# Values scaled among the rotation's turns, scores ahead of maxima and packing, and four smaller moves in an eight-batch transformer block

## The chip, the cores and the metric

One core of a Trainium2 chip runs the program. The metric is the device time of one execution in microseconds. The engines are TensorE (PE in the profile, its weight loads PEld), VectorE (DVE), ScalarE (ACT), GpSimd (POOL) and SyncE (SP), which issues nearly all transfers.

## What is computed

The input x is 8 x 512 x 512, float32. Four layers follow, each added to x after a layer norm of its result:

```python
x = x + ln(lightning_attention(ln(x)))   # 16 query heads, 4 key/value heads of 128, rotation, decay per head
x = x + ln(feed_forward(ln(x)))          # silu(gate) * up, inner 2048, weights (w - 128) * scale
x = x + ln(softmax_attention(ln(x)))     # 32 query heads, 8 key/value heads of 16, rotation, causal
x = x + ln(row_ffn(ln(x)))               # works on the last row, then sigmoid gate over all rows, layer norm
```

The first attention has, per head, q k^T times a table exp(-lam (i - j)), plus a state carried from block to block. The second is the usual softmax attention, with the row maximum subtracted.

## The kernel before, in words

**Precision.** Most products are made of three: every operand is kept as a high and a low part in fp32r. ScalarE copies the high part, VectorE or GpSimd subtracts it from the full value for the low part (`low`, line 1292 on VectorE), and `product` on TensorE multiplies high x high, low x high, high x low.

**Batches are pipelined.** Iteration n (0 to 8) does the first attention of batch n, then its feed-forward; between the pieces of the feed-forward stands the second attention of batch c = n-1; the gate product of batch d = n-2 stands in the first attention. Iteration 8 has no first attention and no feed-forward, and the row network and the last norm come behind it. Each engine's program is written out by hand in one order, with semaphores between them: `fill(bank, emptied)` on TensorE waits until the previous reader of a PSUM bank is through.

**First attention.** Four groups g, each of one key head and four query heads. A group begins with five turns u = 0..4 (keys, then four query heads). In a turn TensorE projects into P0 or P1 (`project`), ScalarE swaps the halves (`swapped`), GpSimd multiplies by the sine table (`sines`, L863), VectorE multiplies by the cosine table (`cosine`, L1344), makes the previous turn's low part (`rope_low`, L1292) and adds the sines (`rotate`, L1350). Behind u = 3 TensorE transposes the key back (`keys_back`), into bank Y0 for g = 0 and E0 otherwise; ScalarE copies it out (kv_hi). For g = 0 `all_values` follows, in banks Y0 and O. Then come the blocks of ten jobs: VectorE scales something into pf (L1407; two buffers), ScalarE copies the high part pT_hi, GpSimd subtracts the low part pT_lo (L875). Jobs 0 and 1 are values times decay (`scaled_values`), read by the state; jobs 2 to 7 are scores times decay (banks T0, T1), 8 and 9 the part from the state. A score product waits for the pf that emptied its bank. In g >= 1 TensorE does the output products of the group before (banks Y0, O; y_acc) ahead of its blocks.

**Fronts and start of the feed-forward.** Then norms, transposes and the q, k, v products of the second attention; VectorE rotates its queries (part 0) and keys (part 1) by `rotate_pairs(c, part, t)`, t = 0..3. The feed-forward has 48 slots, four quarters q of 12. In slots i = 0..7 of a quarter (i = s mod 12) gate (even, bank P0) and up (odd, bank P1) products take turns; ScalarE makes tanh of the gate product, VectorE `silu` (L1568) and `hf` (L1578); in slots 8 to 11 come the down products (Y0, added to y_acc). `product_out(n, s)` is VectorE's part of slot s.

**Second attention, in steps.** From slot 5 five steps stand in three slots: two, two, one. Eight groups of five quads of heads: step i makes scores of quad i mod 5 (`scores`, L2095, banks T0 and T1), VectorE adds the causal mask to the corner (L1551) and takes the maxima (L1558, row_max); only then are T0 and T1 free. A step that needs it also does: `maxima` (L2117, group g at step 6 + 5g, transposes row_max into a spare bank, VectorE copies it as maxT, L1526, SyncE sends it on into QT), `pack_queries` (L2073, step 5g - 2), `pack_keys` (L2081, step 5g - 1), `values_back` (L2134, step 17 + 5g; VectorE divides, rden and y1). Scores in the other orientation with exp (`probs`, L1160), a mask by GpSimd (L897), and products with the values (L2126) come at the start of a step. `layout_high` and `layout_low` put the rotated queries and keys of a group into q_pack and k_pack, two low parts each, on VectorE, at step 5g - 5. The spare bank is P0 in slots with i >= 8, where no gate product runs, and Y0 otherwise. Maxima stand in slots 8, 11, 14, 17, 20, 23, 26 and 29.

**Order of a step on TensorE before:** values, transposed scores, half a slot of feed-forward, maxima, pack_queries, pack_keys, values_back, scores.

**n = 0** also prepares the weights. Each piece is loaded raw, split into high and low (ScalarE, VectorE), and for later batches written to a scratch in DRAM. `first_pieces` gives each piece its place; slots 24 to 31 have the eight pieces of wo1 and of the gate beside eight units and four down pieces per quarter. The fourth quarter has four down pieces.

Of the kernel before, what the change touches and what calls it, by code (L numbers as in the profile page):

```python
# [163 lines left out]
def first_pieces():  # L164
# [98 lines left out]
def build(nc, x, raw_f, raw_i, gate_scale, up_scale, down_scale, rope1_tables, causal, identity_b,  # L263
# [8 lines left out]
    with ExitStack() as ctx:  # L272
# [130 lines left out]
        def keys_bank(g):  # L403

            return "E0" if g else "Y0"
# [428 lines left out]
        def _(pool):  # L834
# [19 lines left out]

            def rope(n, g):
                for u in range(NU):
# [8 lines left out]
                    if g == 2 and u and n:  # L865
                        rstds("pc", n - 1, u - 1)

            def blocks(n, g):
                for k in range(NJOB):
                    lin = (n * KV0 + g) * NRING + k  # L870
                    if k < NRING and lin >= 4:
                        pool.wait_ge(pv.sem, lin - 3)
                    pool.wait_ge(*p_hi.need(n, g, P_HI[k]))
                    if k < NRING:
                        pool.tensor_tensor(pT[1][:, k % 4, :], pf[:, k % 2, :], pT[0][:, k % 4, :].bitcast(F32),  # L875
                                           ALU.subtract).then_inc(*p_lo.hit(n, g, k))
                    else:
                        h = slice(2 * (k - NRING), 2 * (k - NRING) + 2)
# [3 lines left out]
            def clear_pads(c):  # L882
# [6 lines left out]
                pool.memset(k_pack[:, :, 1::2, HD1 + 1:32].bitcast(F32), 0.0).then_inc(*pads.hit(c, 5))  # L889

# [9 lines left out]
            for n in range(NB + 1):  # L900
# [45 lines left out]
                for s in range(SLOTS):  # L946
# [65 lines left out]
        def _(act):  # L1012
# [44 lines left out]

            def rope(n, g):
# [11 lines left out]
                copy(kv[0][:, :], ps[keys_bank(g)][:, :]).then_inc(*rope_hi.hit(n, g, KEYS_AT))  # L1070
# [20 lines left out]
            def blocks(n, g):  # L1091
                for k in range(NJOB):
# [19 lines left out]
                    lin = (n * KV0 + g) * NRING + k  # L1112
                    if k < NRING:
                        if lin >= 4:
                            act.wait_ge(pv.sem, lin - 3)
                        act.wait_ge(*p_f.need(n, g, P_F[k]))
                        copy(pT[0][:, k % 4, :], pf[:, k % 2, :]).then_inc(*p_hi.hit(n, g, P_HI[k]))
# [172 lines left out]
        def _(dve):  # L1290
# [67 lines left out]
            def rope(n, g):  # L1358
                d = n - 2
                dve.wait_ge(*tables_in.need(n))  # L1360
                for u in range(NU):
# [3 lines left out]
                    rotate(n, g, u)  # L1365
                    if g == 0 and d >= 0 and u in (1, 3):
# [139 lines left out]
            def layout_low(c, g):  # L1506
                dve.wait_ge(*q_hi.need(c, g))
                dve.wait_ge(*rot_sum.need(c, 1, NT - 1))
                q_ = q_pack[:, :, :, :].rearrange("p t h e -> p (t h) e")
                low(q_[:, :, 2 * HD1:3 * HD1], R_q[:, g, :, :].rearrange("p t (h d) -> p (t h) d", h=4), q_[:, :, 0:HD1])\  # L1510
                    .then_inc(*q_lo.hit(c, g))
                dve.wait_ge(*k_hi.need(c, g))
                low(k_pack[:, :, 0::2, HD1:2 * HD1], R_k[:, g, :, :].unsqueeze(2).to_broadcast([P, NT, 2, HD1]),
                    k_pack[:, :, 0::2, 0:HD1]).then_inc(*k_lo.hit(c, g))

            def step(c, i):
                at = SLOT_OF[i]
                if prepare_at(i) is not None:
# [897 lines left out]
```

## Time and profile before

| what | value |
|---|---|
| median of three runs | 4074.02 us |
| runs | 4074.05, 4072.42, 4074.02 us |
| the profiled execution | 4069.46 us |
| its span | 4067.7 us |
| mean granted TensorE clock | 0.957 of full speed |
| TensorE busy | 3684.8 us, 91% |
| VectorE busy | 2525.5 us, 62% |
| ScalarE busy | 1505.8 us, 37% |
| GpSimd busy | 1359.4 us, 33% |

The span runs from the first to the last instruction of the profiled execution; its own time is 1.8 us more. Instructions are named by line and tiles: `pf<-ps_T,dec` writes pf and reads ps_T and dec. In a row of the timeline the bracket gives how long the engine stood idle before the instruction and what ended that. x2 joins two equal neighbours.

### The profile page before, as it was taken

Reading aid. Unit: us, or ns where it says so; the run is one execution under the profiler, and the core shown is the slowest. Engines: PE = TensorE matmul, PEld = TensorE weight load, DVE = VectorE, ACT = ScalarE, POOL = GpSimd, SP = SyncE. Lnnn points to the kernel's source line nnn. Section 1 sums busy time; section 2 is a strip of 40 time slices with the busy share of each in tenths; the row PEclk is TensorE's granted clock in tenths of the full one; section 3 lists DMA queues with packets and bytes.
Section 4 is the critical chain, followed back from the end, with each engine's and each line's share of the span. In section 5 each row is a group of like instructions: output and inputs, shape, how many; then the busy total and the mean of one; then the engine's idle time right before and its main releaser. Section 6 shows DMA issues by size and latency. Waiting matters only on the chain. (4 is left out here: it accounts for less than half of the span.)

```text
span 4067.7 us, 51226 instructions
## 1 busy us (share of the span) xinstructions
PE 3684.8 (91%) x18536; PEld 2706.8 (67%) x18536; DVE 2525.5 (62%) x4174; ACT 1505.8 (37%) x2349; POOL 1359.4 (33%) x1674
## 2 busy tenths in 40 slices
PE   6977999999999999999899998999999999977678
PEld 5756776677767776677767776677767776664323
DVE  6654666556674667566664766566664666466347
ACT  4422333434243433434242434434243424315124
POOL 3421452235312551245313541245223541121114
PEclk9988999999999999999999999999999999987789
DMA  6456433254324533254324533353335432332304
GB/s 249 166 215 248 175 129 135 86 205 161 135 84 161 179 122 131 99 205 153 124 94 161 184 106 137 116 204 130 125 105 190 151 134 100 114 106 73 134 14 153
DMA packets 173798, 578.99 MB, mean 142 GB/s; under 512 B 14727, under 2 KB 14983, under 8 KB 168174
## 3 DMA queue, kind: packets, MB, share of 16 engines
q1 hardware_dynamic: 169854, 568.38, 39.3%
q10 hardware_dynamic: 3696, 7.34, 0.5%
q8 instruction: 151, 2.47, 0.3%
q14 instruction: 97, 0.79, 0.1%
HBM read 490.21 MB, written 84.93 MB: 141 GB/s over the span
## 5 line engine op out<-in xcount | busy, mean ns | idle before, releaser
L1892 PE MATMUL ps_P<-XnT_hi,w_ring 128*128 128x512 f32 x3328 | 1084.7, 408 | 60.2 <-DVE silu L1568 24.5
L1892 PEld LDWEIGHTS ps_P<-XnT_hi,w_ring 128*128 128x128 f32 x3328 | 608.5, 192 | 232.1 <-issue 92.3
L1892 PE MATMUL ps_P<-XnT_lo,w_ring 128*128 128x512 f32 x1664 | 659.9, 397 | 0.0
L952 POOL TENSOR_TENSOR hT_lo<-hf,hT_hi 128x512 fp32r<-128x512 f32 x128 | 164.4, 1285 | 935.8 <-ACT hT_hi L1014 935.8
L875 POOL TENSOR_TENSOR pT_lo<-pf,pT_hi 128x512 fp32r<-128x512 f32 x256 | 326.4, 1291 | 358.2 <-ACT pT_hi L1014 358.2
L1160 ACT ACTIVATE probs<-ps_E 128x1024 f32<-128x1024 f32 x320 | 327.5, 1023 | 304.8 <-PE ps_E L2109 304.3
L1558 DVE TENSOR_REDUCE row_max<-ps_T 128x2 fp32r<-128x768 f32 (+3 forms) x448 | 400.1, 917 | 11.0
L1892 PEld LDWEIGHTS ps_P<-XnT_lo,w_ring 128*128 128x128 f32 x1664 | 318.8, 192 | 71.7
L897 POOL TENSOR_SCALAR_AFFINE_SELECT probs<-probs 128x512 f32<-128x512 f32 x256 | 160.0, 637 | 617.2 <-ACT probs L1160 616.1
L1892 PE MATMUL ps_Y<-w_big,hT_hi 128*128 128x512 f32 x896 | 332.0, 417 | 24.8 <-POOL hT_lo L952 11.3
L1551 DVE TENSOR_TENSOR ps_T<-ps_T,mask 128x512 f32<-128x512 f32 (+1 forms) x320 | 187.9, 587 | 230.8 <-PE ps_T L2095 228.9
L863 POOL TENSOR_TENSOR sines<-swapped,sinT 128x512 f32<-128x512 f32 x160 | 212.9, 1331 | 221.3 <-ACT swapped L1014 213.4
L1014 ACT ACTIVATE pT_hi<-pf 128x512 fp32r<-128x512 f32 x256 | 157.2, 630 | 290.3 <-DVE pf L1407 290.3
L1014 ACT ACTIVATE swapped<-ps_P 64x512 f32<-64x512 f32 x320 | 189.8, 593 | 202.4 <-PE ps_P L1892 117.6
L1407 DVE TENSOR_TENSOR pf<-ps_T,dec 128x512 f32<-128x512 f32 x256 | 175.2, 689 | 133.8 <-POOL pT_lo L875 103.3
L1892 PEld LDWEIGHTS ps_Y<-w_big,hT_hi 128*128 128x128 f32 x896 | 169.3, 189 | 99.8 <-issue 17.1
L2095 PE MATMUL ps_T<-KT,QT 64*128 64x256 f32 (+3 forms) x1024 | 166.1, 382 | 72.7 <-DVE row_max L1558 71.5
L1014 ACT ACTIVATE hT_hi<-hf 128x512 fp32r<-128x512 f32 x128 | 80.8, 631 | 311.5 <-DVE hf L1578 311.5
L1568 DVE SCALAR_TENSOR_TENSOR silu<-silu,ps_P 128x512 f32<-128x512 f32 x128 | 87.6, 684 | 167.8 <-ACT silu L1235 167.8
L1344 DVE TENSOR_TENSOR roped<-ps_P,cosT 128x512 f32<-128x512 f32 x160 | 110.3, 689 | 121.9 <-ACT swapped L1014 120.7
L2095 PEld LDWEIGHTS ps_T<-KT,QT 64*128 64x128 f32 x1024 | 84.4, 191 | 149.9 <-DVE row_max L1558 103.5
L2109 PE MATMUL ps_E<-QT,KT 64*128 64x512 f32 (+2 forms) x896 | 154.9, 389 | 25.3 <-ACT probs L1160 25.2
(330 smaller groups left out, 7505.0 us busy)
## 6 DMA issues: line engine op xcount, KB each, us to landing
w_ring<-split_dram SPq DMA_DIRECT2D x412, 512.0 KB, 3.5
w_big<-split_dram SPq DMA_DIRECT2D x64, 2048.0 KB, 7.7
dec<-decay SPq DMA_DIRECT2D x32, 1024.0 KB, 5.0
split_dram<-w_ring SPq DMA_DIRECT2D x58, 512.0 KB, 4.4
split_dram<-w_big SPq DMA_DIRECT2D x36, 512.0 KB, 4.3
wo1w<-split_dram SPq DMA_DIRECT2D x8, 2048.0 KB, 7.6
gatew<-split_dram SPq DMA_DIRECT2D x7, 2048.0 KB, 10.8
X<-raw_f SPq DMA_DIRECT2D x46, 256.0 KB, 4.2
```

Source lines behind the costliest of these rows:

```text
L863: pool.tensor_tensor(sines[:, u % 2, :], swapped[:, u % 2, :], sinT[:, :], ALU.mult)\
L875: pool.tensor_tensor(pT[1][:, k % 4, :], pf[:, k % 2, :], pT[0][:, k % 4, :].bitcast(F32), ALU.subtract).then_inc(*p_lo.hit(n, g, k))
L897: pool.affine_select(out=corner, in_=corner, compare_op=ALU.is_ge, fill=0.0, base=0, pattern=[[0, 4], [1, P]], channel_multiplier=-1).then ...
L952: pool.tensor_tensor(hT[1][:, m % IC, :], hf[:, m % 2, :], hT[0][:, m % IC, :].bitcast(F32), ALU.subtract).then_inc(*h_lo.hit(n, m))
L1014: return act.activation(out_, in_, ACT.Copy)
L1160: act.activation(dst[:, heads_of(ns), :].rearrange("p (b n) i -> p b n i", n=len(ns)), psE[:, :, :].rearrange("p b (n i) -> p b n i", n=le ...
L1407: dve.tensor_tensor(out_, in_, table, ALU.mult).then_inc(*p_f.hit(n, g, P_F[k]))
L1551: dve.tensor_tensor(corner.rearrange("p b n (k s) -> p b (n k) s", s=P) if nh == 1 else corner, corner.rearrange("p b n (k s) -> p b (n k) ...
L1558: last = dve.reduce_max(row_max[:, g % 2, block, heads_of(ns)].rearrange("p (b n) -> p b n", n=len(ns)), psT[:, :, at:at + len(ns) * w].re ...
L1892: last = pe.matmul(dst, stat[s_], mov[m_], start=first_ and k == 0, stop=last_ and k == n - 1, **kw)
L2095: last = pe.matmul(dst[q][:, at + m * w:at + (m + 1) * w], QT[rows_, g % 3, pair, cols(block)], KT[rows_, g % 3, 0:w], start=True, stop=True)
L2109: last = pe.matmul(dst[q][:, at:at + nh * w].rearrange("p (h i) -> p h i", i=w), KT[rows_, g % 3, cols(j)], QT[rows_, g % 3, ns[0]:ns[0] + ...
```

## The change

Six edits:

1. At n = 0 the pieces of wo1 and of the gate go from slots 24 to 31 to slots 38 to 45.
2. `keys_back` uses bank E0 also for g = 0, as long as n < 2.
3. For g >= 1 VectorE's `scaled_values` 0 and 1 stand behind the rotations of turns 2 and 3; ScalarE's and GpSimd's parts of jobs 0 and 1 stand in turns 3 and 4. The blocks then begin with VectorE's two accumulations. GpSimd's roots for "pc" are divided over groups 2 and 3 (turns 1 and 2).
4. `layout_low` runs on GpSimd, in the same steps.
5. In a step TensorE issues `scores` ahead of maxima, pack_queries, pack_keys and values_back. VectorE does mask corner and maxima ahead of the maxT copy and of values_back's division.
6. VectorE's first `product_out` (silu of the first gate product) stands behind the first of the four key rotations instead of behind all four.

```diff
-        if 24 <= s < 28:
-            at.append(("o", s - 24))
-        if 28 <= s < 32:
-            at.append(("g", s - 28))
+        if 38 <= s < 42:
+            at.append(("o", s - 38))
+        if 42 <= s < 46:
+            at.append(("g", s - 42))
...
-        def keys_bank(g):
+        def keys_bank(n, g):
-            return "E0" if g else "Y0"
+            return "E0" if g or n < 2 else "Y0"
...
@@ GpSimd, rope(n, g) @@
-                    if g == 2 and u and n:
-                        rstds("pc", n - 1, u - 1)
+                    if g and u >= 3:
+                        job_low(n, g, u - 3)
+                    if g >= 2 and u in (1, 2) and n:
+                        rstds("pc", n - 1, 2 * (g - 2) + u - 1)
...
@@ GpSimd, slots @@
+                        if s == PREPARE0:
+                            layout_low(c, 0)
                         for i_ in steps_at(s):
+                            if prepare_at(i_) is not None:
+                                layout_low(c, prepare_at(i_))
                             if quad2(i_):
                                 mask_group(c, i_)
...
@@ ScalarE, rope(n, g) @@
+                    if g and u >= 3:
+                        job_high(n, g, u - 3)
...
@@ VectorE, rope(n, g) @@
                     rotate(n, g, u)
+                    if g and u in (2, 3):
+                        scaled_values(n, g, u - 2)
...
@@ VectorE, blocks(n, g) @@
-                for k in range(2):
-                    if g == 0:
+                if g == 0:
+                    for k in range(2):
                         values_low(n, k)
-                    scaled_values(n, g, k)
-                if g:
+                        scaled_values(n, g, k)
+                else:
                     accumulate(n, g - 1, 0)
                     accumulate(n, g - 1, 1)
...
@@ VectorE, start of the feed-forward @@
                     for t in range(NT):
                         rotate_pairs(c, 1, t)
+                        if t == 0 and n < NB:
+                            product_out(n, 0)
...
@@ TensorE, step(n, c, s, i, half) @@
+                if quad1(i):
+                    scores(c, i)
                 if rows_at(i) is not None:
                     maxima(c, rows_at(i), s)
...
                 if back_at(i) is not None:
                     values_back(c, back_at(i), s)
-                if quad1(i):
-                    scores(c, i)
```

The lines with @@ say whose program follows. On VectorE the block of `if quad1(i):` (corner and maxima) moves in the same way to the head of `step`.

## Rows read from the trace of the kernel before

**Rows 1.** The page, section 1: busy us (share of the span) x instructions.

```profile
PE 3684.8 (91%) x18536; PEld 2706.8 (67%) x18536; DVE 2525.5 (62%) x4174; ACT 1505.8 (37%) x2349; POOL 1359.4 (33%) x1674
```

**Rows 2.** Waits of TensorE: who for whom, total us, times, longest.

```profile
PE ps_T L2095 <- DVE row_max L1558: 71.5, 88, 2.3
PE ps_T L1892 <- DVE pf L1407: 70.1, 54, 2.2
```

**Rows 3.** Three stretches: busy us per engine, then clock, DMA share, GB/s.

```profile
1540.00:1545.00 5.00, 4.43 (x13) 3.54 (x14) 1.70 (x4) 0.90 (x2) 1.27 (x1) 0.66 1.03 397
1629.00:1634.00 5.00, 3.27 (x20) 2.38 (x20) 3.01 (x6) 2.86 (x4) 3.09 (x4) 1.00 0.00 0
1853.00:1859.00 6.00, 4.20 (x11) 2.87 (x12) 3.35 (x5) 1.38 (x3) 4.67 (x4) 0.72 0.00 0
```

**Rows 4.** Timeline, first silu of a batch: start, duration, line, tiles, [idle before].

```profile
1535.64 0.69 ACT L1235 ACTIVATE silu<-ps_P,ghalf 128x512 f32<-128x512 f32 x1 [5.08 <-PE ps_P L1892]
...
1539.74 0.68 DVE L1568 SCALAR_TENSOR_TENSOR silu<-silu,ps_P 128x512 f32<-128x512 f32 x1
...
1540.57 0.70 PE L1892 MATMUL ps_P<-XnT_hi,w_ring 128*128 128x512 f32 x2 [2.30 <-DVE silu L1568]
```

**Rows 5.** Timeline, a group's blocks (second group of the fifth batch).

```profile
1850.49 0.69 DVE L1292 TENSOR_TENSOR qT_lo<-roped,qT_hi 128x512 fp32r<-128x512 f32 x1 [0.70 <-ACT qT_hi L1014]
...
1851.10 1.29 DVE L1407 TENSOR_TENSOR pf<-v,ident_dec 128x512 f32<-128x512 f32 x2
...
1852.66 2.49 POOL L875 TENSOR_TENSOR pT_lo<-pf,pT_hi 128x512 fp32r<-128x512 f32 x2 [4.01 <-ACT pT_hi L1014]
...
1854.80 0.50 PE L1892 MATMUL ps_T<-qT_hi,kT_hi 128*128 128x512 f32 x1 [1.90 <-DVE pf L1407]
...
1859.43 0.39 PE L1892 MATMUL ps_Y<-w_big,oT_hi 128*128 128x512 f32 x1
```

**Rows 6.** Timeline, one turn of the rotation: VectorE and GpSimd.

```profile
1879.59 1.29 POOL L863 TENSOR_TENSOR sines<-swapped,sinT 128x512 f32<-128x512 f32 x1 [1.39 <-ACT swapped L1014]
...
1880.16 1.27 DVE L1292 TENSOR_TENSOR kT_lo<-roped,kT_hi 128x512 fp32r<-128x512 f32 x1
...
1880.84 0.64 POOL L845 TENSOR_TENSOR var_eps<-moments,eps 128x1 f32<-128x1 f32 x1
...
1881.36 0.68 DVE L1350 TENSOR_TENSOR roped<-roped,sines 128x512 f32<-128x512 f32 x1
...
1882.27 0.69 DVE L1344 TENSOR_TENSOR roped<-ps_P,cosT 128x512 f32<-128x512 f32 x1 [0.24 <-ACT swapped L1014]
```

**Rows 7.** Timeline, slots 11 and 12 of a feed-forward.

```profile
1587.98 1.22 DVE L1558 TENSOR_REDUCE row_max<-ps_T 128x4 fp32r<-128x1024 f32 x1
...
1588.76 0.56 PE L2117 MATMUL ps_P<-identr,row_max 128*128 128x128 f32 x4
...
1589.26 0.50 PE L2095 MATMUL ps_T<-KT,QT 64*128 64x384 f32 x4
...
1589.72 0.67 DVE L1526 CAST maxT<-ps_P 4x512 fp32r<-4x512 f32 x1
...
1590.32 0.68 DVE L1551 TENSOR_TENSOR ps_T<-ps_T,mask 128x512 f32<-128x512 f32 x1
...
1590.53 0.70 PE L1892 MATMUL ps_P<-XnT_hi,w_ring 128*128 128x512 f32 x2 [0.49 <-DVE maxT L1526]
...
1591.03 1.29 DVE L1558 TENSOR_REDUCE row_max<-ps_T 128x2 fp32r<-128x768 f32 x2
```

**Rows 8.** VectorE on q_pack, all batches: ns min/median/max, first and last start.

```profile
L1292 DVE TENSOR_TENSOR q_pack<-R_q,q_pack x64: 412/435/1095, 633.3 to 3732.1; 128x256 fp32r<-128x256 f32 x64
```

**Rows 9.** Quarters two to four of the first feed-forward, columns as in rows 3.

```profile
289.00:331.00 42.00, 36.34 (x148) 28.27 (x147) 18.82 (x29) 11.96 (x20) 5.15 (x4) 0.96 0.61 226
331.00:388.00 57.00, 40.17 (x142) 30.13 (x142) 27.09 (x44) 16.78 (x28) 8.03 (x12) 0.85 0.72 276
388.00:425.00 37.00, 36.15 (x165) 28.75 (x164) 17.84 (x29) 9.54 (x16) 5.14 (x4) 1.00 0.51 185
```

**Rows 10.** Timeline of TensorE, the wait ahead of the first batch's values.

```profile
50.16 0.77 PE L1892 MATMUL ps_Y<-w_big,XnT_hi 128*128 128x512 f32 x1 [8.53 <-ACT kv_hi L1014]
```

More of the change, by code:

```diff
@@ L864, in rope @@
                         .then_inc(*sine_done.hit(n, g, u))
[L865 to L866 removed]
+                    if g and u >= 3:
+                        job_low(n, g, u - 3)
+                    if g >= 2 and u in (1, 2) and n:
+                        rstds("pc", n - 1, 2 * (g - 2) + u - 1)
             def blocks(n, g):
[L869 to L873, printed above, removed]
+                for k in range(2 if g else 0, NJOB):
                     if k < NRING:
[L875 to L876 removed]
+                        job_low(n, g, k)
                     else:
+                        pool.wait_ge(*p_hi.need(n, g, P_HI[k]))
                         h = slice(2 * (k - NRING), 2 * (k - NRING) + 2)
@@ L1056, in rope_high, with job_high @@
                     .then_inc(*rope_hi.hit(n, g, UNIT_AT[u]))
+            def job_high(n, g, k):
+                lin = (n * KV0 + g) * NRING + k
+                if lin >= 4:
+                    act.wait_ge(pv.sem, lin - 3)
+                act.wait_ge(*p_f.need(n, g, P_F[k]))
+                copy(pT[0][:, k % 4, :], pf[:, k % 2, :]).then_inc(*p_hi.hit(n, g, P_HI[k]))
             def rope(n, g):
@@ L1111, in blocks @@
                                 .then_inc(*o_hi.hit(n, g, h))
-                    lin = (n * KV0 + g) * NRING + k
                     if k < NRING:
[L1114 to L1117, printed above, removed]
+                        if k >= 2 or g == 0:
+                            job_high(n, g, k)
                     else:
@@ L1504, in rotate_pairs @@
                 dve.tensor_tensor(dst, dst, b_.rearrange("p (g e) -> p g e", g=KV1), ALU.add).then_inc(*rot_sum.hit(c, part, t))
[L1506 to L1514, printed above, removed]
             def step(c, i):
                 at = SLOT_OF[i]
-                if prepare_at(i) is not None:
-                    layout_low(c, prepare_at(i))
+                if quad1(i):
+                    g, x_ = quad1(i)
+                    if c * KV1 + g >= 2:
+                        dve.wait_ge(rows_mm.sem, c * KV1 + g - 1)
+                    dve.wait_ge(*pads.need(c, 0))
+                    nh = len(STEPS1[x_][0][1])
+                    corner = psT[:, :, :].rearrange("p b (n s) -> p b n s", n=nh)[:, :, :, (4 // nh - len(STEPS1[x_])) * P:512 // nh]
+                    dve.wait_ge(*score1.need(c, g, x_))
+                    dve.tensor_tensor(corner.rearrange("p b n (k s) -> p b (n k) s", s=P) if nh == 1 else corner,
+                                      corner.rearrange("p b n (k s) -> p b (n k) s", s=P) if nh == 1 else corner,
+                                      mask[:, :].unsqueeze(1).unsqueeze(1).to_broadcast([P, 2, max(nh, len(STEPS1[x_])), P]), ALU.add)\
+                        .then_inc(*corner_done.hit(c, g, x_))
+                    dve.wait_ge(*corner_done.need(c, g, x_))
+                    for block, ns, at_ in STEPS1[x_]:
+                        w = (block + 1) * P
+                        last = dve.reduce_max(row_max[:, g % 2, block, heads_of(ns)].rearrange("p (b n) -> p b n", n=len(ns)),
+                                              psT[:, :, at_:at_ + len(ns) * w].rearrange("p b (n s) -> p b n s", s=w), AX_X)
+                    last.then_inc(*max_done.hit(c, g, x_))
                 g = rows_at(i)
@@ L1745, in _ @@
                             step(c, i)
-                    if n < NB and s % 12 < 8:
+                    if n < NB and s % 12 < 8 and (s or c < 0):
                         product_out(n, s)
```

41 lines of the change are left out of this document (19 added, 22 removed).

## The prediction, on record before the changed kernel ran

> **What bounds the kernel now.** I read the page first, then the list of waits of TensorE, then single stretches of the timeline. TensorE is busy for 3684.8 us, 91% of the span, and the next engine 62% [rows 1], so only what TensorE waits for, and how fast it runs, can move the time. The waits for row_max and for pf, 70 us each, lead its list [rows 2]; the change goes at both, and at a wait for silu that comes once a batch. Second reading, the granted clock: the stretch behind the 2.30 us silu wait was granted 0.66 and that behind a 1.90 us pf wait 0.72, while behind a 1.73 us wait at 1631.15 it stayed 1.00 [rows 3]. At 2.4 GHz a mean of 0.66 means that part of the stretch ran at 1.2 GHz. The price of such a spell: 5 us x 0.34 = 1.7 us, or 6 us x 0.28 = 1.7 us [rows 3]. So a wait of about two microseconds costs itself and 1.7 us more, and one below about 1.7 us only itself.
>
> **The first silu moved up (seven batches).** tanh of the first gate product ends at 1536.33, but VectorE comes to silu at 1539.74, behind all four key rotations, and TensorE, which wants the same bank, stands 2.30 us until 1540.57 [rows 4]. The first rotation takes about 0.85 us (four lie between 1536.33 and 1539.74), so silu then runs from 1537.2 to 1537.9, ahead of 1538.27, when TensorE is ready for it. I leave 0.3 us of the wait. The three rotations behind it end 0.68 us later and have only a packing many microseconds later as reader. Gain 2.0 + 1.6 of clock = 3.6 us, x7 = **-25** (bounds -14, without the clock, and -28).
>
> **Scaled values among the turns (21 groups with g>=1).** Now a group begins when the last qT_lo is there, at 1851.18; then two scalings of 0.65, two POOL subtractions of 1.25, and only then the scaled scores that the third score product (job 4) waits for: TensorE waits 1.90 for pf and begins the outputs at 1859.43, 8.2 us after the start [rows 5]. After the change the scalings and POOL's first two subtractions stand in turns 2 to 4. What do turns have free? Per turn VectorE does a cosine 0.69, a low 1.27 and a rotation 0.68, and ahead of the next cosine, at 1882.27, it stands idle for 0.24 [rows 6]. The low is 1.27 and not 0.69 as it is when POOL is idle [rows 5, 6]: it starts at 1880.16 inside POOL's sines and ends 0.55 after these. And POOL's tiny var_eps, issued at 1880.84, lasts until VectorE's low is over. The rows read best as turns taken, one whole operation after the other, not as two slower operations. Then each of two job lows (1.25) and two scalings (0.65) goes into the queue of both engines: I set them into turns 2 to 4 and got the last low 2.7 us later than now. TensorE waits these 2.7 at the start and then no longer for pf at job 4; outputs begin 4.8 us behind the last low at full clock, or 5.8 with a half-speed spell: 7.5 to 8.5 against 8.2. That is -0.7 to +0.3 per group; the wait of 2.7 is of those that cost clock, so I take the upper half: **0** (bounds -69, if the turns' slack swallowed all but 0.15 of it, and +17, at 0.8 more per group). The Trainium skill, page "SBUF — State Buffer", section "SBUF: two separate sides", says that VectorE and GpSimd share one port pair as an exclusive lock: a VectorE operation with two SBUF inputs and a GpSimd operation that reads SBUF never overlap, the first to start keeps it to its end. By that the delay would be the 2.7 taken here, and the rule speaks against this part of the change. The trace agrees as far as it goes, with its low that ends 0.55 us behind POOL's operation. POOL's variance roots move from g=2 to g=2 and 3, same count: nothing, covered by the same turns (if not covered, 0.64 [rows 6] a few times per batch, within the bound).
>
> **Scores ahead, maxima and maxT behind.** In slot 11 the scores come at 1589.26, just after their condition, the reduction that ends at 1589.20 (1587.98 + 1.22 [rows 7]). Maxima stand ahead of them and cover that wait. Afterwards the scores can't start sooner: TensorE idles there, and maxima follow. On VectorE corner and reduction (0.68, 1.29) now come ahead of the maxT copy (0.67), which frees bank P0; the next slot's gate product needs P0. Today it waits 0.49 and starts at 1590.53. By the new order: corner 1589.8, reduction to 1591.8, maxT to 1592.5, product at 1592.6: 2.1 us later, of which the next scores' small wait gives back 0.2, and the idle above adds 0.4: 2.3. The same holds at slot 23: only in these two do maxima use P0 right before a gate product; elsewhere (slots 8, 14, 17, 20, 26, 29) nobody wants the bank at once. Packing, behind the scores, gets its operands' banks later; subtractions for it now run on POOL, twice as long per element (1.25 against 0.69 for the same shape [rows 5]), with a mask ahead of them. I add 0.25 and 0.8 for the two groups where the packing then waits on them, and take off 0.3 where a score comes sooner. Per batch: 2 x 2.3 + 1.0 = 5.6, x7 = **+39**. Each new wait is about 2.0 to 2.1, where the rows show half-speed spells [rows 3]; with chance 0.8 each, and one more at half that weight, 1.8 spells x 1.7 = 3.0 per batch, x7 = **+21**. Bounds: +10 (the packing alone) and +75.
>
> **Layout lows to POOL in the last pass.** With no feed-forward, VectorE is the bound of n=8, and 8 x 0.435 leave it [rows 8], and as many of the keys' lows, of half the elements: 5.5 us, **-5** (bounds -8 and 0). In the other batches VectorE's time for it is the gap that TensorE does not see.
>
> **Weights at n=0.** The third quarter (331:388) takes 57 us for nearly the TensorE work (40.2 us busy, against 36.3) that the second does in 42, with the clock at 0.85 [rows 9]. In it 20 weight pieces are split (8 units, 4 of the down weights, 8 of wo1 and gate), in the second 12. Eight of them (wo1, gate) go to slots 38 to 45, into the fourth quarter, which has 4 now and then 12, as the third will. If a quarter of 12 pieces costs what the second costs, the third falls to 41 or 42 us (-16 of its 57.8), and the fourth (388:425, 37 us [rows 9]) rises towards 42: +5. **-11** (bounds -14 and -6).
>
> **Bank of the first key transposes (n<2).** TensorE waits 8.53 us for kv_hi at 50.16 [rows 10], because all_values wants the same bank; with E0 it goes at once, until it needs v_lo, which VectorE gives only behind the last qT_lo of the turns. By my placing that takes back half of the wait. **-4** (bounds -7, 0); n=1: nothing, as the next wait, v_lo, ends where it did.
>
> **Sum:** -25 + 0 + 39 + 21 - 5 - 11 - 4 = **+15**. The profiled execution took 4069.5 us (span 4067.7), so 4084.5 by it; the median of the runs is 4.6 higher, 4074.0, hence **4089**.
>
> **Rivals.**
> 1. Turns absorb the scalings, faster. If only the two scalings' own 1.3 us delay the last low instead of 2.7, each block begins 1.4 earlier and keeps its clock more often (0.5): 1.9 x 21 = -40, time 4049. It decides from the point where the last qT_lo comes less than 2.4 us later than today. For it: the last low of a group runs at 0.69 [rows 5]. Against: the low and var_eps that wait out the other engine [rows 6]. Chance 0.20.
> 2. Scores first gives what it seems to promise, faster: row_max waits of 71.5 [rows 2] fall by a third, and P0's wait stays near 0.5, since the reduction finishes earlier. -24 instead of +60: 4005 to 4030. Against: the condition of the scores is met only at 1589.20. Chance 0.10.
> 3. The new waits keep the clock at 1.00, as the 1.73 us wait did [rows 3]: without the 21, 4068. Chance 0.20, no change that can be told.
> 4. The turns cost more: POOL's queue makes sines late, and both the last low and the clock suffer: +0.8 x 21, time 4106. Chance 0.12.
> 5. The main case: 0.38.
>
> **Numbers.** About 0.2% (8 us) is what a measurement of this kernel can tell from nothing: 4066 to 4082. Faster 0.30 (1, 2), same 0.20 (3), slower 0.50 (4, 5). The range reaches from rival 1's to the top of rival 4, with what the upper bound of the scores' part adds: 4040 to 4112; the likeliest case alone has 4078 to 4100.
>
> **What would show it.** Right: a wait of TensorE for maxT near 2 us at slots 12 and 24 of each batch; silu's wait at the batch's start gone, with the clock at 1.00 behind it; qT_lo of the last turn some 2.7 us later and no pf wait of 1.9; slots 12 to 23 of n=0 near 41 us. Wrong: lows of 0.69 beside POOL's new work, maxT waits unchanged, or a silu wait that has only moved to hf.

## The result, and the profile after

The changed kernel takes 4124.8 us (4118.9 to 4127.4, four runs) against 4074.0 of before in the same comparison: ratio 1.0121, 95% interval 1.0104 to 1.0139, so it is 50.8 us slower. The forecast was 4089 with a range up to 4112: the side was right, the size was not. The profiled execution took 4118.9 us (span 4117.2), 49.5 more in the span than before. Here are two lines of its page: the busy times, and the granted clock in forty equal slices of the span.

```profile
PE 3724.4 (90%) x18536; PEld 2700.7 (66%) x18536; DVE 2547.2 (62%) x4046; ACT 1505.3 (37%) x2349; POOL 1456.5 (35%) x1802
...
PEclk8989999999999999999999999999999999986789
```

Against [rows 1] TensorE's busy time is 40 us up with the same number of matmuls: they ran longer, in part because more of the time is at half speed (below). Its list of waits (who for whom, total us, times, longest):

```profile
PE ps_T L1908 <- DVE qT_lo L1318: 67.1, 24, 3.9
PE ps_T L2111 <- DVE row_max L1552: 63.0, 107, 2.3
...
PE ps_P L1908 <- DVE maxT L1561: 26.2, 14, 1.9
...
PE ps_T L1908 <- DVE pf L1435: 20.4, 20, 2.2
...
PE ps_P L1908 <- DVE silu L1584: 5.9, 7, 1.7
```

Against [rows 2] the pf wait fell from 70.1 to 20.4, as meant, and a wait for the last qT_lo stands in its place: 67.1 us in 24 waits, 2.4 to 2.9 us each in batches 2 to 8 and 3.8 to 3.9 in the first. maxT is new among the long ones at 14 x 1.87. The wait for silu is nearly gone (5.9; it was 24.5).

Where the time went is read best by stages. The table gives the length of each stretch from the starts of TensorE's projections and of the feed-forward's products, in us; a group holds its turns and its blocks, the last column of a batch runs to the next batch's first projection.

```
fifth batch        groups 1   2     3    4+fronts | quarters 1    2      3   4 and rest | sum
before              53.4  40.9  40.9  73.8        | 57.9  75.6  62.8  49.4    | 454.5
after               51.7  40.0  41.3  75.1        | 57.8  79.7  64.7  49.4    | 459.6
after, third batch  53.3  41.3  41.2  73.4        | 56.3  81.5  64.5  49.4    | 460.8

               first batch  batches 2 to 8  from there to the end | TensorE idle, half-speed time (granted clock) in 2 to 8
before            408.3        3146.0         493.9               | 173.8, 105.8 in 31 spells
after             399.6        3196.9         500.9               | 186.3, 153.6 in 36 spells
```

(In the second table batches 2 to 8 begin with the second batch's first projection and end where the last gate or up product of the eighth batch starts. The column behind runs from there to the end of TensorE's last product. A spell is a stretch at half speed without a break.) The loss lies in the second and third quarter and in the last pass; in the first quarter silu's gain and a new loss cancel out. In batches 2 to 8 TensorE idles only 12.5 us more, but 47.8 us more of its time run at half speed, which is worth half as much, 23.9. Together they are 36 of the 50.9 us. The other 15 are neither gaps nor half speed; their cause wasn't found.

### The profile page after: what moved, and what is told of

Its sections match the earlier page's. It is cut to its first block, busy times and chain, and to the rows that moved or that the text cites. A ratio compares the mean times of both kernels' runs of the same rounds, so it can differ in the third digit from the quotient of the medians.

```text
span 4117.2 us, 51225 instructions
## 1 busy us (share of the span) xinstructions
PE 3724.4 (90%) x18536; PEld 2700.7 (66%) x18536; DVE 2547.2 (62%) x4046; ACT 1505.3 (37%) x2349; POOL 1456.5 (35%) x1802
## 4 chain that ended last, share of the span: by engine, by line
PE 59%; DVE 22%; issue 7%; POOL 4%; ACT 4%; DMA 3%; SPq 1%; DVEq 0%; ACTq 0%; POOLq 0%
PE ps_P L1908 20%; PE ps_Y L1908 9%; PE ps_E L1908 6%; PE ps_T L1908 4%; PE ps_O L2142 4%; PE ps_O L1908 3%; PE ps_T L2111 3%; PE ps_E L2125 2%; DVE row_max L1552 2%; DVE roped L1376 2%; DVE ps_T L1545 2%; DVE qT_lo L1318 2%; DVE pf L1435 2%; DVE stats L1342 1%; POOL X L853 1%
## 5 line engine op out<-in xcount | busy, mean ns | idle before, releaser
L860 POOL TENSOR_TENSOR pT_lo<-pf,pT_hi 128x512 fp32r<-128x512 f32 x256 | 343.5, 1354 | 395.7 <-ACT pT_hi L1034 395.7
L871 POOL TENSOR_TENSOR sines<-swapped,sinT 128x512 f32<-128x512 f32 x160 | 225.0, 1406 | 171.8 <-ACT swapped L1034 165.8
L2125 PE MATMUL ps_E<-QT,KT 64*128 64x512 f32 (+2 forms) x896 | 163.7, 409 | 26.7 <-ACT probs L1186 26.5
L2142 PE MATMUL ps_O<-probs,V 128*32 128x512 f32 (+3 forms) x2048 | 177.0, 466 | 0.0
```

What stands on the lines that cost most here:

```text
L871: pool.tensor_tensor(sines[:, u % 2, :], swapped[:, u % 2, :], sinT[:, :], ALU.mult)\
L2125: last = pe.matmul(dst[q][:, at:at + nh * w].rearrange("p (h i) -> p h i", i=w), KT[rows_, g % 3, cols(j)], QT[rows_, g % 3, ns[0]:ns[0] + ...
L2142: last = pe.matmul(dst[at:at + 32, j * P:S], V1[:, j, g, :], probs_of(j)[:, m, :], start=(j == 0), stop=(j == NT - 1), skip_group_check=True)
```

## The experiments

Each kernel ran against the kernel before on the same chip; differences are of medians. Each took four to ten executions; the edits shown are cut to what matters (... stands for lines left out).

### The silu edit alone, and silu behind the third rotation

```diff
                         rotate_pairs(c, 1, t)
+                        if t == 0 and n < NB:     # f_only; t == 2 in f_third
+                            product_out(n, 0)
```

> The kernel before with the silu edit alone. My account: the silu wait of 2.30 us and the half-speed spell behind it go, the first quarter of the feed-forward falls from 57.9 to 54.3 us in each of seven batches: -25 us, 4049. The rival (clock spell only moves to another place): -14 us, 4060, with the first quarter at 55.9.

> The kernel before with silu behind the third key rotation instead of the first: the wait is left at 1.4 to 1.5 us instead of 2.3 or 0. If half-speed spells follow only waits near 2 us, the spell goes with it and the first quarter is near 55.4 us: -17 (4057). If the spell stays it is 57.0: -6 (4068).

The first took 4045.1, -27.5 us (ratio 0.9932, 0.9917 to 0.9947). Its first quarter is 54.3 us instead of 57.9. The second took 4056.0, -15.2 us (0.9962, 0.9950 to 0.9975), with a first quarter of 55.5. Timeline and then the stretch behind the wait (busy times of the engines, then the clock) in the second kernel:

```profile
1538.21 0.70 PE L1894 MATMUL ps_P<-XnT_hi,w_ring 128*128 128x512 f32 x2 [1.44 <-DVE silu L1568]
```

```profile
1538.00:1545.00 7.00, 6.59 (x32) 5.37 (x32) 3.56 (x11) 2.34 (x5) 1.29 (x1) 1.00 1.04 403
```

The wait is 1.44 and the clock stays at 1.00, where [rows 3] had 0.66 behind 2.30. So 0.86 of the 2.4 us that the quarter lost is wait, and the other 1.5 is the clock. This term of the forecast (-25, of it 1.6 us of clock per batch) came within 2.5 us, and here its two shares can be told apart.

The second kernel shows one thing more. Its second quarter takes 77.1 to 77.2 us in all seven batches, where before it took 75.6, and each time it holds one spell of 3.4 us that wasn't there before. In the fifth batch it comes behind a wait of 1.73 us for probs, at 2077.68; in the kernel before the same wait is 1.71, at 2085.62, and no spell follows. So in the second kernel the spell left the silu wait and another came elsewhere, as the rival in the expectation of `f_only` had it. In the first kernel none came: there the second quarter stays at 75.6.

### Scaled values among the turns, alone

> The kernel before with scaled values among the turns alone. The account by turns taken (port held by whole operations): last qT_lo 2.7 us later, blocks 3.5 us shorter, +0.4 us per group in steady batches and about +6 us at n=0: +8 to +14, 4082 to 4088. The rival (turns absorb the scalings): 1.9 us less per group, -40, 4034.

```diff
                     rotate(n, g, u)
+                    if g and u in (2, 3):
+                        scaled_values(n, g, u - 2)    # VectorE; ScalarE's and GpSimd's parts in u = 3, 4
```

It took 4072.4, -0.1 us (0.9995, 0.9985 to 1.0004): no difference, as the sum said, and below the +8 to +14 of the expectation. Why is seen in the turns of the changed kernel (fifth batch, second group, turns 2 to 4 and the head of the blocks):

```profile
1854.85 1.48 POOL L871 TENSOR_TENSOR sines<-swapped,sinT 128x512 f32<-128x512 f32 x1 [1.43 <-ACT swapped L1034]
...
1855.70 1.18 DVE L1318 TENSOR_TENSOR qT_lo<-roped,qT_hi 128x512 fp32r<-128x512 f32 x1
...
1856.29 1.74 POOL L860 TENSOR_TENSOR pT_lo<-pf,pT_hi 128x512 fp32r<-128x512 f32 x1
...
1856.80 1.77 DVE L1376 TENSOR_TENSOR roped<-roped,sines 128x512 f32<-128x512 f32 x1
...
1858.03 1.70 POOL L871 TENSOR_TENSOR sines<-swapped,sinT 128x512 f32<-128x512 f32 x1
...
1858.50 1.78 DVE L1435 TENSOR_TENSOR pf<-v,ident_dec 128x512 f32<-128x512 f32 x1
...
1861.15 1.47 POOL L860 TENSOR_TENSOR pT_lo<-pf,pT_hi 128x512 fp32r<-128x512 f32 x1 [1.42 <-ACT pT_hi L1034]
...
1861.40 1.76 DVE L1376 TENSOR_TENSOR roped<-roped,sines 128x512 f32<-128x512 f32 x1
...
1863.86 0.69 DVE L1318 TENSOR_TENSOR qT_lo<-roped,qT_hi 128x512 fp32r<-128x512 f32 x1 [0.69 <-ACT qT_hi L1034]
...
1864.61 0.50 PE L1908 MATMUL ps_T<-qT_hi,kT_hi 128*128 128x512 f32 x1 [2.59 <-DVE qT_lo L1318]
...
1866.41 0.51 PE L1908 MATMUL ps_T<-qT_hi,kT_hi 128*128 128x512 f32 x1
```

From 1854.85 to 1863.16 operations of VectorE are held up beside operations of GpSimd: GpSimd's operation at 1856.29 ends at 1858.03, and the rotation beside it, 0.68 by itself [rows 6], takes 1.77 and ends 0.54 behind it. The scaling takes 1.78 beside the sines of 1.70, and the next rotation 1.76 beside a subtraction of 1.47. The last low comes late enough that TensorE waits 2.59 at 1864.61. The pf wait of 1.90 [rows 5] is then 0.14 (the 1866.41 row follows at once). The delay was forecast at 2.7, and the waits of batches 2 to 8 are 2.4 to 2.9. Over the whole execution the mean rotation is 0.99 us, where it was 0.68. GpSimd's fuller queue is not what makes the last low late: VectorE's waits for sines are 24.3 us in all, and 24.6 before, and VectorE has no idle time between the first row shown and 1863.16. By the lock that the forecast cited from the Trainium skill ("SBUF — State Buffer", "SBUF: two separate sides") one operation waits for the whole of the other; these rows agree, except that VectorE's operation ends only about 0.55 behind GpSimd's, less than its own 0.68.

### The same on VectorE and ScalarE alone

This is the test of that reading: GpSimd's two subtractions go back to the head of the blocks, and its roots for "pc" to their old place. It was run together with the weights, layout and silu edits, beside a kernel with these three edits alone.

```diff
             # GpSimd, rope(n, g)
-                    if g and u >= 3:
-                        job_low(n, g, u - 3)
```

> Added to it: scaled values among the turns on VectorE and ScalarE alone; GpSimd's two subtractions stay at the head of the blocks. If the lock between the two engines makes the last qT_lo late, it comes only some 1.0 to 1.4 us later instead of 2.7, and the pf wait of 1.9 falls too, since GpSimd can start at once: blocks 0.5 to 1.5 us shorter each, -10 to -30 against the run without: 3980 to 4000. If VectorE's own time is at fault, the last qT_lo is 2.7 late here too and the run is no faster.

> The same without the bank of the first key transposes. My forecast gave that edit -4. The traces since show only another wait in its place (w_big 8.3 for kv_hi 8.5 at n=0, v_lo 6.5 for 2.6 + 2.0 at n=1): no difference beyond noise, or 2 us faster without it: 4010.

> All edits but the order of scores and the scaled values among the turns. If the turns' part is neutral (as it was alone), this equals the run without the order alone, 4022. If it costs once silu no longer covers the clock spell behind the last group, or at n=0, where a group took 3.9 us longer in it, this is 8 to 15 us faster: 4010.

With GpSimd left out of the turns: 3977.9 (-93.3; 0.9774, 0.9760 to 0.9789). Without the scaled values' edit: 4017.6 (-53.7; 0.9871, 0.9856 to 0.9885), and with the bank edit added 4017.7 (-53.5). So the edit is worth 40 us in this form and about nothing in the form of the change (the run below, with it, is -54.8). The second and third group of a batch take 38.7 to 38.9 and 38.1 to 38.2 instead of 39.6 to 41.3. The timeline of the fifth batch, second group:

```profile
1798.05 0.68 DVE L1370 TENSOR_TENSOR roped<-roped,sines 128x512 f32<-128x512 f32 x1
...
1798.66 0.68 DVE L1429 TENSOR_TENSOR pf<-v,ident_dec 128x512 f32<-128x512 f32 x1
...
1799.01 1.49 POOL L863 TENSOR_TENSOR sines<-swapped,sinT 128x512 f32<-128x512 f32 x1 [1.43 <-ACT swapped L1028]
...
1807.47 0.50 PE L1902 MATMUL ps_T<-qT_hi,kT_hi 128*128 128x512 f32 x1 [1.29 <-DVE qT_lo L1312]
```

The rotation and the scaling behind it run at their own 0.68; GpSimd has only its sines, and the last low makes TensorE wait 1.29 instead of 2.59. Half-speed time in batches 2 to 8 falls from 92.2 us (27 spells) to 30.7 (9), and idle time from 144.0 to 126.7: of 48 us (3108.7 to 3060.6) 17 are waits and 31 are clock. In the first batch the edit costs 9.1 in these two executions, which leaves the 40. That is the price of the forecast's first rival, with a wait near the 1.3 us that it names. The edit could have gained it, if GpSimd's part hadn't gone along.

The bank edit made no difference. In the changed kernel TensorE waits 8.25 us at the first batch for w_big (its low half is split by VectorE), where it waited 8.53 for kv_hi, and at the second batch the wait for v_lo is 6.5 instead of waits of 2.6 and 2.0.

### The order of scores, alone and split

```diff
                 # TensorE, step, in e_only and e_pe_only
+                if quad1(i):
+                    scores(c, i)
                 if rows_at(i) is not None:
                     maxima(c, rows_at(i), s)
...
                     values_back(c, back_at(i), s)
-                if quad1(i):
-                    scores(c, i)
```

In `e_only` VectorE's order changes in the same way, in `e_pe_only` it stays. In `e_maxima` TensorE's order is packing, values_back, scores, maxima, so that only maxima and the maxT copy go behind. In `e_packs` it is maxima, scores, packing, values_back.

> The kernel before with the order of scores alone, on TensorE and on VectorE. My account: first quarter +2.0, second +5 (P0's wait for maxT and the clock spell), third +2 per batch, and the pass without feed-forward +7 to +12: +70, 4144. The rival (the loss is the GpSimd lows of the packs): no more than the maxT waits, 2 x 1.4 x 7 = +20, 4094.

> The order of scores on TensorE alone; VectorE keeps maxT and the division ahead of the corner and the maxima. If the maxT copy behind corner and maxima is what costs in slots 12 and 24, the wait falls from 1.9 to about 0.9 us, its spells go, and the sum is +30 to +40 (4104 to 4114), with the last pass still +7. If it is the packing behind the scores, little changes against the run with both orders: +60 or more.

> Only maxima and the maxT copy behind the scores; packing and the division stay ahead. If P0's wait for maxT is the larger part of the loss, this has the second quarter at +5 and the sum near +60 (4133); if the packing is, it has only +2 x 1.4 us of wait and two spells of 1.7 us in a batch, +40 (4113) or less.

> Only packing and values_back (with VectorE's division) behind the scores; maxima and maxT stay ahead. Account: the 1.04 us of the query packing no longer fill VectorE's reduction, TensorE idles 0.6 us there and the packing, and the next product's wait for QT, come on top, 1.4 us in each of 8 groups plus 0.5 for the keys: up to 13 us per batch, less where slack takes it; +50 to +80 (4123 to 4153), all three quarters and the last pass. The rival: maxima carry the loss, this is +15.

Alone it takes 4188.2: **+115.6** (1.0279, 1.0264 to 1.0295), far more than the +70 that I expected. On TensorE alone 4213.6, +141.0 (1.0343, 1.0328 to 1.0359), where I expected +30 to +40. Only maxima behind: 4153.1, +76.1 (1.0191, 1.0176 to 1.0207). Only packing and values_back behind: 4119.8, +42.8 (1.0108, 1.0093 to 1.0123). The two halves add up to 118.9. I had expected about +60 for the first half and +50 to +80 for the second, each with the rival that the other half carries the loss; both halves carry it.

Maxima first. Slots 11 and 12 in the changed kernel, and the clock there (against [rows 7]):

```profile
1591.56 0.51 PE L2111 MATMUL ps_T<-KT,QT 64*128 64x384 f32 x4 [0.33 <-DVE row_max L1552]
...
1592.00 0.66 PE L2133 MATMUL ps_P<-identr,row_max 128*128 128x128 f32 x4
1592.21 0.70 DVE L1545 TENSOR_TENSOR ps_T<-ps_T,mask 128x512 f32<-128x512 f32 x1
...
1592.94 1.29 DVE L1552 TENSOR_REDUCE row_max<-ps_T 128x2 fp32r<-128x768 f32 x2
...
1594.15 0.67 DVE L1561 CAST maxT<-ps_P 4x512 fp32r<-4x512 f32 x1
...
1594.96 1.19 PE L1908 MATMUL ps_P<-XnT_hi,w_ring 128*128 128x512 f32 x2 [1.87 <-DVE maxT L1561]
```

```profile
1593.00:1601.00 8.00, 6.13 (x21) 4.26 (x18) 3.81 (x6) 2.05 (x2) 1.85 (x3) 0.57 0.45 157
1864.00:1870.00 6.00, 5.25 (x22) 3.99 (x23) 3.82 (x7) 1.78 (x4) 2.54 (x2) 1.00 0.00 0
```

Scores start when the reduction is done; maxima follow, but their copy waits in VectorE's queue for corner and reduction, and TensorE stands 1.87 us for bank P0, as forecast (2.0 to 2.1). What was not: the clock behind it. 0.57 over 8 us is 3.4 us, twice the price that I took from [rows 3]. This is one of the dearer places. Over all 14 waits for maxT, each of 1.87 us, the 8 us behind hold 4.0 us at half speed on average, worth 2.0, and behind two of them there are none. The second window holds the opposite: behind a wait of 2.59 it stayed 1.00, as behind 3 of the 21 waits for qT_lo in batches 2 to 8. Length of the wait alone doesn't tell which one is followed by a spell.

In the kernel with TensorE's order alone the copy goes first:

```profile
1624.07 0.50 PE L2095 MATMUL ps_T<-KT,QT 64*128 64x384 f32 x4 [0.35 <-DVE row_max L1558]
...
1625.27 0.68 DVE L1526 CAST maxT<-ps_P 4x512 fp32r<-4x512 f32 x1 [0.66 <-PE ps_P L2117]
...
1625.88 0.68 DVE L1551 TENSOR_TENSOR ps_T<-ps_T,mask 128x512 f32<-128x512 f32 x1
...
1626.10 0.70 PE L1892 MATMUL ps_P<-XnT_hi,w_ring 128*128 128x512 f32 x2 [0.50 <-DVE maxT L1526]
```

TensorE's wait for P0 is 0.50 as in [rows 7]. But VectorE stood idle for maxima until 1625.27, and the corner, whose scores were there at 1624.57, starts at 1625.88. The loss moved into the loop of scores and reductions: 233 us of idle time in batches 2 to 8 against 204 in `e_only`, and 104 us of waits for row_max against 53. My expectation had left VectorE's queue behind the waiting copy out. So if TensorE's order is changed, VectorE's must be too, and even then it loses.

Packing. The fourth scores of a group, first in the kernel before (packing at 1594.61, scores at 1595.58 without a wait), then in the kernel with both orders:

```profile
1594.61 0.60 PE L2073 MATMUL ps_Y<-ident_dec,q_pack 128*128 128x128 f32 x4
...
1595.58 0.49 PE L2095 MATMUL ps_T<-KT,QT 64*128 64x512 f32 x2
```

```profile
1596.16 0.51 PE L2095 MATMUL ps_T<-KT,QT 64*128 64x512 f32 x2 [0.62 <-DVE row_max L1536]
...
1596.60 0.66 PE L2073 MATMUL ps_Y<-ident_dec,q_pack 128*128 128x128 f32 x4
...
1597.10 0.60 PE L2073 MATMUL ps_P<-ident_dec,q_pack 128*128 128x128 f32 x4
...
1598.53 0.70 PE L1892 MATMUL ps_P<-XnT_hi,w_ring 128*128 128x512 f32 x2 [0.83 <-ACT QT L1014]
```

In the old order the packing, about 1 us, filled the time until the reduction was done. Now TensorE idles 0.62, packs behind the scores, and the product behind needs the bank that ScalarE is still reading: 0.83 more. It is the last pass that shows the shift of work best. Scores four to five, kernel before and changed kernel:

```profile
3692.88 0.79 PE L2095 MATMUL ps_T<-KT,QT 64*128 64x512 f32 x2
...
3696.97 0.50 PE L2095 MATMUL ps_T<-KT,QT 64*128 64x512 f32 x2
```

```profile
3738.01 0.79 PE L2111 MATMUL ps_T<-KT,QT 64*128 64x512 f32 x2 [0.45 <-DVE row_max L1552]
3738.74 1.12 PE L2089 MATMUL ps_Y<-ident_dec,q_pack 128*128 128x128 f32 x4
3739.64 1.06 PE L2089 MATMUL ps_P<-ident_dec,q_pack 128*128 128x128 f32 x4
3740.64 3.21 PE L2142 MATMUL ps_O<-probs,V 128*32 128x512 f32 x16
...
3744.35 0.40 PE L2111 MATMUL ps_T<-KT,QT 64*128 64x512 f32 x2
```

Before, packing stands ahead of 3692.88, in the shadow of VectorE's reduction, and 4.09 us later come the next scores, with the products with the values (2.4 us) between. Afterwards the packing (1.9 us) and these products (3.2) both stand between two scores, 6.34 us, and VectorE is idle for 4.25 us ahead of the next corner. The interval ahead of these scores fell only from 3.16 to 3.01. Scores are issued earlier once, and the next ones later by all that was put behind them.

### The layout lows on GpSimd, alone

> The kernel before with the layout lows on GpSimd alone. In the old order the scores stand in VectorE's queue behind the lows, which wait for ScalarE's high parts; taking them out helps the last pass by 5 us and perhaps each batch by 0.5: -5 to -12, 4060 to 4068. The rival (GpSimd's slower lows delay the packing): +10, 4083.

```diff
             # VectorE, step(c, i)
-                if prepare_at(i) is not None:
-                    layout_low(c, prepare_at(i))
```

It took 4050.0: **-27.1** (0.9937, 0.9922 to 0.9952), well beyond what I gave it. In the kernel before and in this one, the first scores of a group:

```profile
1554.32 0.50 PE L2095 MATMUL ps_T<-KT,QT 64*128 64x256 f32 x4
...
1554.84 0.42 DVE L1292 TENSOR_TENSOR q_pack<-R_q,q_pack 128x256 fp32r<-128x256 f32 x1
...
1555.18 0.28 DVE L1292 TENSOR_TENSOR k_pack<-R_k,k_pack 128x128 fp32r<-128x128 f32 x1
...
1555.38 0.69 DVE L1551 TENSOR_TENSOR ps_T<-ps_T,mask 128x512 f32<-128x512 f32 x1
...
1557.39 0.50 PE L2095 MATMUL ps_T<-KT,QT 64*128 64x384 f32 x4 [1.00 <-DVE row_max L1558]
```

```profile
1558.24 0.51 PE L2095 MATMUL ps_T<-KT,QT 64*128 64x256 f32 x4
...
1558.88 0.70 DVE L1553 TENSOR_TENSOR ps_T<-ps_T,mask 128x512 f32<-128x512 f32 x1 [1.06 <-PE ps_T L2095]
...
1559.81 0.74 POOL L895 TENSOR_TENSOR q_pack<-R_q,q_pack 128x256 fp32r<-128x256 f32 x1
```

The lows stand in VectorE's queue ahead of the corner: scores began at 1554.32, the corner at 1555.38, 1.06 later, and TensorE waits 1.00 for the reduction, at 1557.39. Without them the corner starts 0.64 behind the start of the scores, and GpSimd does the lows later, at 1559.81. The wait for row_max in batches 2 to 8 falls from 40.1 to 23.4 us. That VectorE was busy with it "in the gap that TensorE doesn't see" was wrong: a gap of VectorE's is free only if the operation ends before the loop comes round to it. This one ends behind the start of the scores, since it needs the high parts that ScalarE makes, the first of them only at 1554.10.

### All but the order

> The changed kernel with the old order of scores, maxima and packing on both engines; all five other edits stay. If the order of scores is what makes the change slower, this beats the kernel before: silu -27, weights and bank -10 to -15, scaled values between 0 and +10, last pass -5: about -38, 4035. The rival (the GpSimd lows are at fault too): 4060 or more.

```diff
             # TensorE, step, of the changed kernel (and VectorE's step in the same way)
-                if quad1(i):
-                    scores(c, i)
                 if rows_at(i) is not None:
                     maxima(c, rows_at(i), s)
...
                     values_back(c, back_at(i), s)
+                if quad1(i):
+                    scores(c, i)
```

It took 4022.2: **-54.8** (0.9865, 0.9849 to 0.9882). So the order costs 103 us in the changed kernel (4124.8), and the other five edits together are faster than before by more than 1%. (The two profiled executions are only 89 apart: that of `all_but_e` lies 8 above its median, that of the changed kernel 6 below.) Silu's 27.5 and the layout's 27.1 make up the whole of it; for weights, bank and the scaled values no more than a few microseconds are left. With weights, layout and silu alone it is the same: -53.7, where the last two by themselves add up to -54.6. The weights' edit wasn't run by itself. In the first batch of `adf` the third quarter did fall, from 57.8 to 39.9, and the fourth and the stretch behind it rose by 5, as forecast; the whole first batch took 393.7 there, 14.6 less than before. But in seven kernels whose edits don't touch it the first batch took from 403.6 to 410.2 us (408.3 before), and the medians show none of the gain. So what the edit is worth stays open.

### In the whole change, and the best version

> The changed kernel, but GpSimd's subtractions of jobs 0 and 1 back at the head of the blocks. If their place in the turns is all that undid the scaled values' gain, this gains what it gave without the order of scores: 45 us, 4080. If half-speed spells of the slots follow from those of the blocks, more or less by 10.

> The changed kernel, but maxima and the maxT copy ahead of the scores again; packing and values_back stay behind. Alone, maxima cost 76 of the order's 115 us and packing 43. If they add in the whole change too (102 for both there), maxima are about 65 of it: 4060. If it is P0's wait for maxT alone with its spells, 14 x (1.4 + 1.7) = 43: 4082.

> Weights later, layout lows on GpSimd, silu moved up, old order of scores, and scaled values among the turns on VectorE and ScalarE alone, for all batches but the first. In the first batch that edit cost 9 us (groups of 47.2 instead of 41.5 to 43.1), in the others it gave 6.9 each: against the run with it everywhere (3978) -9, 3969.

```diff
             # best: VectorE, rope, and ScalarE's job_high in the same way
-                    if g and u in (2, 3):
+                    if n and g and u in (2, 3):
                         scaled_values(n, g, u - 2)
```

The first of these has the edit to GpSimd's turns shown for `adf_c_light`, the second the step's order of `e_packs`. The best version has the old order and GpSimd's old place, and leaves the bank edit out too.

With GpSimd's subtractions back: 4067.9, -5.7 (0.9987, 0.9977 to 0.9996), 57 us below the changed kernel, where I expected 45. With maxima ahead: 4064.3, -9.3 (0.9979, 0.9967 to 0.9990), 60.5 below it, as the shares of 76 and 43 said (65), and not the 43 of P0's wait with its spells alone. Either of the two, undone, turns the change from slower into a few microseconds faster than before.

The best version takes 3973.4 us, **-100.1** (0.9749, 0.9733 to 0.9765). Its wait for the last low, 67.1 us in the changed kernel:

```profile
PE ps_T L1903 <- DVE qT_lo L1312: 23.5, 21, 1.5
```

It leaves the first batch in the old order. That I had priced at 9 us from one execution's groups; its gain against 3977.9 is 4.5, with intervals that overlap, and the first batch itself took 401.1 against 402.8. So the 9 us did not show; most of them can be the spread of the first batch.

```
us                     first batch  batches 2 to 8  to the end | idle    half speed in 2 to 8
before                    408.3        3146.0        493.9    | 173.8   105.8 (31 spells)
silu alone                403.6        3122.3        496.1    | 158.8    88.7 (26)
layout alone              404.5        3132.3        491.8    | 157.5   112.6 (33)
order alone               407.9        3255.0        507.8    | 203.5   221.8 (59)
TensorE's order alone     409.1        3258.1        525.6    | 233.1   146.8 (43)
all but the order         404.6        3114.1        491.6    | 156.2    95.6 (26)
best                      401.1        3059.2        491.8    | 124.9    30.7 (9)
```

The order alone costs 109 us in batches 2 to 8: 30 are idle time, 58 are half of 116 us more at half speed, and 21 remain, which I didn't trace. In the changed kernel the order costs 83 in the same batches (3196.9 against 3114.1 without it): 30 are idle time, 29 clock, and 24 remain in the same way.

## Why the prediction was wrong, point by point

The step that failed is the price of the scores' new order, +60 in the forecast and +103 in the whole change.

- **Silu moved up**: forecast -25, measured -27.5. Right, and in its shares too: the first quarter fell by 3.6 to 3.8 us in each of the seven batches, where the sum had 3.6.
- **Scaled values**: forecast 0, measured -0.1 alone. Right in mechanism and size: the last low 2.4 to 2.9 late, the long pf wait gone. The run with GpSimd's part taken out of the turns shows that what eats the gain is GpSimd's share, and not VectorE's time. The sum counted 21 groups, but the edit holds for n=0 too, and the wait comes 24 times.
- **Scores ahead**: forecast +60, measured +115.6 alone and +103 with the rest. P0's wait was placed and sized rightly (14 times, 1.87 for 2.0 to 2.1). In batches 2 to 8 the 60 (39 of waits, 21 of clock) even agree with what the order added to idle time (30) and to the clock (29). What failed is the rest: (a) the packing was given 1.0 us per batch and costs 5.5 (38.8 us in batches 2 to 8 of `e_packs`), since it lost its cover in the first quarter too, where I had put nothing; (b) 24 us in batches 2 to 8 are neither gaps nor half speed, and the sum has no term for them; their cause is open; (c) the last pass had no term for the order at all. The spells behind P0's wait were a smaller error: 2.0 us per wait on average, where the 21 us of the sum make 1.5. The 1.0 for the packing isn't what its parts give either: 0.25 + 0.8 - 0.3 is 0.75.
- **Layout lows**: forecast -5, all of it in the last pass, measured -27.1. "The gap that TensorE does not see" was wrong: the layout gives 13.7 us in batches 2 to 8 of the profiled execution, and 2.1 in the last pass.
- **The last pass**: forecast -5, measured +7.0. There the order takes 9.3 (500.9 against 491.6 without it). I had priced only the layout, though this is the pass without any feed-forward to cover the order.
- **Weights and bank**: forecast -15, and the medians show next to nothing. The bank gave nothing, since another wait stood right behind it: for w_big, and not for v_lo as I had it. In the profiled executions the first batch is shorter by 8.7 in the changed kernel and by 14.6 in `adf`, beside a spread of 6.6 among kernels without the edit. The sign that I named for the weights has the wrong slots, too: the quarter that fell to 39.8 is slots 24 to 35, and not 12 to 23.
- By stages: first batch -8.7 (forecast -15), batches 2 to 8 +50.9 (+35), the end +7.0 (-5): +49 against +15. By edits: the order is dearer by 43, weights, bank and all that the single runs leave over come out 18 above the forecast, and against them stand 22 of the layout and 2.5 of silu.

That the side came out right is in part luck. The layout's 22 us were missed in the other direction; with them, and with the rest as I had it, the forecast would have been 4067, no difference. Of the rivals the fourth ended nearest (4106), but its mechanism was not at work: the sines don't come late, and the turns' edit alone costs nothing. Rival 2 had the waits for row_max fall by a third; with the order alone they rose from 71.5 to 85.6 us.

The range was too narrow by its own terms. The top of rival 4 and the upper bound of the scores' part make 4106 + 15 = 4121, and it ends at 4112. That bound, +75, did not let the order alone be dearer: it was taken around my own schedule of slot 11 and not around the whole loop of a group.

## What to carry to other kernels

Where two engines pass a bank to and fro, work that stood ahead of the waiting instruction cost nothing here up to the length of the wait; put behind it, it lengthened the next round. So sum, for each interval between two uses, what stands in it on both engines, and move work only from the longer interval to the shorter one. When a part of a chain is moved into another stage, move each engine's share as a decision of its own: here VectorE's share was worth 40 us, and GpSimd's took them back.

## What was not expected of the hardware

- The clock follows more than the wait before it. Behind 1.44 us at 1538.21 it stayed at full speed; behind 1.87 us in slot 12 it fell to a mean of 0.57 for 8 us, and behind 2.59 us at 1864.61 it stayed at 1.00. The same wait for probs, 1.71 and 1.73 us, is followed by no spell in the kernel before and by one in `f_third`. In batches 2 to 8 the best version has 9 spells and the order alone 59, with 125 and 204 us of idle time: half-speed time went from 31 to 222 us while the idle time didn't double.
- An operation of VectorE (rotation or scaling) that alone takes 0.68 us took 1.76 to 1.78 beside a GpSimd operation of 1.47 to 1.74, and ended 0.54 to 0.55 us behind it in each case. VectorE so lost about 1.1 us each time.
